# Splitting the q and k projections into fp16 halves straight from the matmul bank, in a two-layer graph attention kernel

## What is computed

```python
h = jnp.maximum(_layernorm(x, axis=-1), 0.0)
x = x + _L0_gnn_ref(h, adj, Wq, bq, Wk, bk, Wv, bv, beta)
h = jnp.maximum(_layernorm(x, axis=-1), 0.0)
x = x + _L1_gnn_ref(h, adj, Wq, Wk, Wv, bv, Wo, bo)
```

## Time and profile before

| | |
|---|---|
| median of 3 runs | 2788.24 us (2787.83 to 2789.91) |
| span of the profiled execution, first to last instruction | 2786.6 us |
| PE busy | 2492.9 us, 89% |
| VectorE busy | 2035.5 us, 73% |
| ScalarE busy | 2045.4 us, 73% |
| GpSimd busy | 1205.5 us, 43% |
| DMA, share of 16 engines | about a third, 90 GB/s |

### The profile page before, as it was taken

The page is one execution under the profiler, slowest core; times in us unless marked ns, Lnnn a source line. Parts: engine busy times, 40 slices in busy tenths (PEclk is TensorE's granted clock), DMA queues, the critical chain, the costliest instruction groups (busy, mean ns, idle before and its releaser), DMA issues.

```text
span 2786.6 us, 78169 instructions
## 1 busy us (share of the span) xinstructions
PE 2492.9 (89%) x20772; PEld 1447.7 (52%) x20772; DVE 2035.5 (73%) x10864; ACT 2045.4 (73%) x7824; POOL 1205.5 (43%) x1543
## 2 busy tenths in 40 slices
PE   3699999999999999999999999999999999999976
PEld 2355555555555555555555555555555555555543
DVE  3477777777777777777777777777777777777756
ACT  2577777777777777777777777777777777777765
POOL 1344444454444444444444444444444444444431
PEclk8899999999999999999999999999999999999988
DMA  3333333333333333333333333333333333333321
GB/s 118 90 89 87 93 94 87 95 102 86 88 96 86 94 103 86 86 97 87 94 102 88 85 99 86 94 100 89 83 99 88 95 98 90 82 99 91 78 55 45
DMA packets 164279, 251.27 MB, mean 90 GB/s; under 512 B 29776, under 2 KB 114768, under 8 KB 163920
## 3 DMA queue, kind: packets, MB, share of 16 engines
q1 hardware_dynamic: 163920, 248.11, 33.7%
HBM read 71.83 MB, written 25.17 MB: 35 GB/s over the span
## 4 chain that ended last, share of the span: by engine, by line
PE 45%; ACT 17%; DVE 16%; issue 16%; POOL 3%; SPq 1%; ACTq 1%; DVEq 1%; DMA 0%; POOLq 0%
PE job_bank L765 21%; ACT probs L479 12%; PE pt_bank L792 9%; PE o_bank L807 4%; PE misc_bank L832 4%; DVE neg L575 4%; PE score_bank L781 2%; PE misc_bank L846 2%; DVE stats L603 2%; ACT h_hi L516 2%; ACT probs_t L493 2%; PE misc_bank L868 1%; ACT qk L531 1%; DVE h_lo L700 1%; POOL part_lo L420 1%
## 5 line engine op out<-in xcount | busy, mean ns | idle before, releaser
L479 ACT ACTIVATE probs<-neg,neg_max 128x128 f32<-128x128 f32 x3072 | 1185.5, 390 | 9.4 <-DVE neg_max L575 9.4
L493 ACT ACTIVATE probs_t<-pt_bank 128x512 f32<-128x512 f32 x768 | 458.2, 597 | 567.7 <-PE pt_bank L792 516.5
L406 POOL TENSOR_TENSOR rstd<-shift_var,minus_half 128x1 f32<-128x1 f32 x256 | 152.2, 595 | 1020.3 <-DVE shift_var L612 1020.3
L479 ACT ACTIVATION_READ_ACCUMULATOR probs<-neg,neg_max 128x1 f32 x3072 | 583.9, 190 | 0.0
L792 PE MATMUL pt_bank<-ident,probs 128*128 128x128 f32 x3072 | 476.1, 278 | 57.5 <-ACT probs L479 42.9
L420 POOL TENSOR_TENSOR part_lo<-qk,part_hi 128x512 f16<-128x512 f32 x384 | 459.1, 1205 | 115.6 <-DVE part_hi L710 115.6
L792 PEld LDWEIGHTS pt_bank<-ident,probs 128*128 128x128 f32 x3072 | 362.7, 141 | 238.9 <-ACT probs L479 154.8
L765 PE MATMUL job_bank<-h_hi,w_hi 128*128 128x512 f16 x1152 | 441.4, 383 | 43.9 <-ACT qk L531 25.4
L765 PE MATMUL job_bank<-h_lo,w_hi 128*128 128x512 f16 x1152 | 438.5, 381 | 0.0
L765 PE MATMUL job_bank<-h_hi,w_lo 128*128 128x512 f16 x1152 | 438.0, 380 | 0.0
L575 DVE CUSTOM_DVE_ANT_0 neg<-score_bank,bias 128x128 f32<-128x128 f32 x1536 | 352.8, 285 | 103.3 <-issue 98.6
(11 more groups left out here) (69 smaller groups left out, 3949.8 us busy)
## 6 DMA issues: line engine op xcount, KB each, us to landing
stack<-part_hi SPq DMA_DIRECT2D x1024, 96.0 KB, 2.2
stack<-part_lo SPq DMA_DIRECT2D x512, 96.0 KB, 2.2
x_norm<-in_x SPq DMA_DIRECT2D x32, 768.0 KB, 4.5
x_res<-in_x SPq DMA_DIRECT2D x32, 768.0 KB, 4.7
out_x<-result SPq DMA_DIRECT2D x128, 192.0 KB, 1.9
adj<-in_adj SPq DMA_DIRECT2D x64, 256.0 KB, 2.9
stack<-in_L_gnn_Wq SPq DMA_DIRECT2D x2, 576.0 KB, 8.1
stack<-in_L_gnn_Wk SPq DMA_DIRECT2D x2, 576.0 KB, 8.9
```

What stands on the lines that cost most here:

```text
L406: pool.tensor_tensor(rstd[:, :], shift_var[:, b % 2, 1:2], minus_half[:, :], ALU.pow).then_inc(rstd_done, 1)
L479: last = act.activation(probs[c % 2][:, h, :], neg[c % 2][:, h, :], ACT.Exp, bias=neg_max[:, b, first + h:first + h + 1], scale=-1.0, accu ...
L493: act.activation(probs_t[c % 2][:, :, :].rearrange("p h q -> p (h q)"), pt_bank[c % 2][:, :], ACT.Copy).then_inc(probs_t_ready, 1)
```

## The change

q and k go from the bank to their halves without the fp32 copy. ACT writes the high half itself (scale and bias in the same instruction, output fp16), and DVE makes the low half in one instruction from the bank and the high half. GpSimd has no part in it. The bank is therefore free only when DVE is done: PE now waits on `part_lo_ready`. The wait for the landed copies moves from DVE to ACT. ACT no longer waits for the buffers of two jobs before. So that both engines form the same value in layer 0, where a bias is added, the weights of q and k are scaled by 16 instead of 256 and the factor is carried on: q and k are 16 times too large, the bias columns are scaled by 16, the scores are scaled back by 1/(256 sqrt(32)) inside the instruction of line 575, and beta and the mask value are scaled up to match. The setup gets two small DVE instructions more.

```diff
@@ GpSimd
-            def low_part(u, j):
-                n = u.n * 2 * KC + j
-                pool.wait_ge(part_hi_ready, n + 1)
-                pool.tensor_tensor(part_lo[j // KC][:, j % KC, :], qk32[j % 2][:, :],
-                                   part_hi[j // KC][:, j % KC, :], ALU.subtract).then_inc(part_lo_ready, 1)
...
-                    if p.project is not None and 2 <= s < 2 + 2 * KC:
-                        low_part(p.project, s - 2)
@@ ScalarE, slot j + 1
                         act.wait_ge(job_done, u.n * JOBS + (j + 1))
-                        if some(n - 1):
-                            act.wait_ge(part_hi_ready, n - 1)
-                        if some(n - 1):
-                            act.wait_ge(part_lo_ready, n - 1)
+                        if j % KC == 0 and some((u.half + u.parity) * STACK_DMAS * 16):
+                            act.wait_ge(stack_in[t][1 - u.parity], (u.half + u.parity) * STACK_DMAS * 16)
                         if u.layer == 0:
-                            last = act.activation(qk32[j % 2][:, :], job_bank[j % 2][:, :], ACT.Identity,
-                                                  scale=scale, bias=cols[:, j % KC:j % KC + 1])
+                            last = act.activation(part_hi[t][:, j % KC, :], job_bank[j % 2][:, :], ACT.Identity,
+                                                  scale=1.0, bias=b_cols[t][:, j % KC:j % KC + 1])
                         else:
-                            last = act.activation(qk32[j % 2][:, :], job_bank[j % 2][:, :], ACT.Copy, scale=scale)
-                        last.then_inc(qk32_ready, 1)
+                            scale = (SCALE[1] if t == 0 else 1.0) / W_SCALE
+                            last = act.activation(part_hi[t][:, j % KC, :], job_bank[j % 2][:, :], ACT.Copy,
+                                                  scale=scale)
+                        last.then_inc(part_hi_ready, 1)
@@ VectorE, slot j + 1
-                        dve.wait_ge(qk32_ready, u.n * 2 * KC + (j + 1))
-                        if j % KC == 0 and some((u.half + u.parity) * STACK_DMAS * 16):
-                            dve.wait_ge(stack_in[j // KC][1 - u.parity], (u.half + u.parity) * STACK_DMAS * 16)
-                        dve.tensor_copy(part_hi[j // KC][:, j % KC, :], qk32[j % 2][:, :]).then_inc(part_hi_ready, 1)
+                        t = j // KC
+                        dve.wait_ge(part_hi_ready, u.n * 2 * KC + (j + 1))
+                        if u.layer == 0:
+                            last = dve.scalar_tensor_tensor(part_lo[t][:, j % KC, :], job_bank[j % 2][:, :],
+                                                            b_cols[t][:, j % KC:j % KC + 1], part_hi[t][:, j % KC, :],
+                                                            ALU.add, ALU.subtract)
+                        else:
+                            scale = (SCALE[1] if t == 0 else 1.0) / W_SCALE
+                            last = dve.scalar_tensor_tensor(part_lo[t][:, j % KC, :], job_bank[j % 2][:, :], scale,
+                                                            part_hi[t][:, j % KC, :], ALU.mult, ALU.subtract)
+                        last.then_inc(part_lo_ready, 1)
@@ TensorE, first third of job j
-                        pe.wait_ge(qk32_ready, u.n * 2 * KC + (j - 1))
+                        pe.wait_ge(part_lo_ready, u.n * 2 * KC + (j - 1))
@@ VectorE, scores and setup
-                        scale=-1.0, scalar=HUGE, op0=ALU.add, op1=ALU.min,
+                        scale=(-1.0 / SCORE0 if u.layer == 0 else -1.0), scalar=HUGE, op0=ALU.add, op1=ALU.min,
...
-            dve.tensor_scalar(bq_cols[:, :], bq_raw[:, :], SCALE[0], None, ALU.mult).then_inc(bq_ready, 1)
+            for t in range(2):
+                dve.tensor_scalar(b_cols[t][:, :], b_raw[t][:, :], QK0_SCALE, None, ALU.mult).then_inc(cols_ready, 1)
+            dve.tensor_scalar(beta_all[:, :], beta_raw[:, :], SCORE0, None, ALU.mult).then_inc(cols_ready, 1)
+            dve.wait_ge(cols_ready, 3)
```

More of the change, by code:

```diff
@@ L46 @@
 SCALE = (float(HEAD) ** -0.5, float(DIM) ** -0.5)
+QK0_SCALE = 16.0
+SCORE0 = QK0_SCALE * QK0_SCALE / SCALE[0]
 class Unit:
@@ L175, in build @@
         carried_p, carried_v = count(), count()
+        beta_raw = sb("beta_raw", [P, 1])
         beta_all = sb("beta_all", [P, 1])
-        bq_raw = sb("bq_raw", [P, KC])
-        bq_cols = sb("bq_cols", [P, KC])
-        bk_cols = sb("bk_cols", [P, KC])
+        b_raw = [sb(f"b_raw{t}", [P, KC]) for t in range(2)]
+        b_cols = [sb(f"b_cols{t}", [P, KC]) for t in range(2)]
         bv_rows = [sb(f"bv_rows{m}", [P, DIM]) for m in range(2)]
@@ L201, in build @@
         h_lo = [sb(f"h_lo{b}", [P, KC, TOK], F16) for b in range(2)]
-        qk32 = [sb(f"qk32{b}", [P, TOK]) for b in range(2)]
         part_hi = [sb(f"part_hi{t}", [P, KC, TOK], F16) for t in range(2)]
@@ L245, in build @@
         half_ready = sem("half_ready")
-        bq_ready = sem("bq_ready")
+        cols_ready = sem("cols_ready")
         weight_turned = sem("weight_turned")
@@ L264, in build @@
         job_done = sem("job_done")
-        qk32_ready = sem("qk32_ready")
         part_hi_ready = sem("part_hi_ready")
@@ L308, in _ @@
         def _(sp):
-            sp.dma_start(bq_raw[:, :], b0q.rearrange("(c p) -> p c", p=P),
+            sp.dma_start(b_raw[0][:, :], b0q.rearrange("(c p) -> p c", p=P),
                          allow_slow_non_contiguous=True).then_inc(consts_in, 16)
-            sp.dma_start(bk_cols[:, :], b0k.rearrange("(c p) -> p c", p=P),
+            sp.dma_start(b_raw[1][:, :], b0k.rearrange("(c p) -> p c", p=P),
                          allow_slow_non_contiguous=True).then_inc(consts_in, 16)
-            sp.dma_start(beta_all[:, :], beta[0].partition_broadcast(P)).then_inc(consts_in, 16)
+            sp.dma_start(beta_raw[:, :], beta[0].partition_broadcast(P)).then_inc(consts_in, 16)
             sp.dma_start(x_norm[:, :, :], x_groups[0]).then_inc(x_norm_in, 16)
@@ L460, in _ @@
                 act.wait_ge(weight_in[m], 16)
-                act.activation(w_hi[m][:, :, :], staging(m), ACT.Copy, scale=W_SCALE).then_inc(w_hi_ready, 1)
+                act.activation(w_hi[m][:, :, :], staging(m), ACT.Copy,
+                               scale=QK0_SCALE if m < 2 else W_SCALE).then_inc(w_hi_ready, 1)
             for m in range(3, 7):
@@ L467, in _ @@
                                    scale=W_SCALE).then_inc(w_hi_ready, 1)
-            act.wait_ge(bq_ready, 1)
+            act.wait_ge(cols_ready, 3)
             act.wait_ge(consts_in, 96)
@@ L521, in phase @@
                         u, j = p.project, s - 1
-                        n = u.n * 2 * KC + j
+                        t = j // KC
                         act.wait_ge(job_done, u.n * JOBS + (j + 1))
-                        if some(n - 1):
-                            act.wait_ge(part_hi_ready, n - 1)
-                        if some(n - 1):
-                            act.wait_ge(part_lo_ready, n - 1)
-                        scale = (SCALE[u.layer] if j < KC else 1.0) / W_SCALE
+                        if j % KC == 0 and some((u.half + u.parity) * STACK_DMAS * 16):
+                            act.wait_ge(stack_in[t][1 - u.parity], (u.half + u.parity) * STACK_DMAS * 16)
                         if u.layer == 0:
-                            cols = bq_cols if j < KC else bk_cols
-                            last = act.activation(qk32[j % 2][:, :], job_bank[j % 2][:, :], ACT.Identity,
-                                                  scale=scale, bias=cols[:, j % KC:j % KC + 1])
-                        else:
-                            last = act.activation(qk32[j % 2][:, :], job_bank[j % 2][:, :], ACT.Copy, scale=scale)
-                        last.then_inc(qk32_ready, 1)
+                            last = act.activation(part_hi[t][:, j % KC, :], job_bank[j % 2][:, :], ACT.Identity,
+                                                  scale=1.0, bias=b_cols[t][:, j % KC:j % KC + 1])
+                        else:
+                            scale = (SCALE[1] if t == 0 else 1.0) / W_SCALE
+                            last = act.activation(part_hi[t][:, j % KC, :], job_bank[j % 2][:, :], ACT.Copy,
+                                                  scale=scale)
+                        last.then_inc(part_hi_ready, 1)
             run_phases(act, phase)
@@ L547, in _ @@
             dve.wait_ge(consts_in, 96)
-            dve.tensor_scalar(bq_cols[:, :], bq_raw[:, :], SCALE[0], None, ALU.mult).then_inc(bq_ready, 1)
+            for t in range(2):
+                dve.tensor_scalar(b_cols[t][:, :], b_raw[t][:, :], QK0_SCALE, None, ALU.mult).then_inc(cols_ready, 1)
+            dve.tensor_scalar(beta_all[:, :], beta_raw[:, :], SCORE0, None, ALU.mult).then_inc(cols_ready, 1)
+            dve.wait_ge(cols_ready, 3)
             for m in range(3):
                 dve.wait_ge(w_hi_ready, m + 1)
```

(6 more changed lines are left out.)

1 line of the change is left out of this document (added).

## The result

The changed kernel takes **2832.7 us** (median of 4, 2830.26 to 2836.19) against 2788.03 us for the kernel before in the same session: ratio **1.0162**, 95% interval 1.0148 to 1.0177. It is 1.6% slower. The forecast was 2819 us, with a range of 2786 to 2843. The granted clock was 0.985 of full speed on average in both profiled executions, so it has no part in the difference.

A forecast was written before the change was run, and what follows sets the result against it. PE, busy 89% of the span, was taken as the bound. Losses of 0.36 (phase A) and 0.67 (phase B) give 1.03 us per period, x 28 is 29, plus 2 outside the loop: 2819 us, range 2786 to 2843.

The forecast's parts named there:

- behind h_lo: Phase A, job 1: the bank comes free at 1064.81 against PE's start at 1064.45, so PE loses 0.36 us.
- job 4 hidden: Phase A: job 4 meets the same order, but PE waits for the exponentials in slot 6 anyway, so no loss.
- job 0: Phase B: PE loses about 0.2 us because job 0's bank comes free later.
- job 2's half behind VectorE's statistics: Phase B, slot 3: VectorE reaches job 2 late, so PE's job 4 starts 1.67 us later than before.
- ScalarE's half in fp16: ScalarE's fp16 output was to cost nothing: h_hi in fp16 took 0.474 us, o_t in fp32 0.471.
- the moved wait for the landed copies: On ScalarE instead of VectorE: to cost nothing, as the copies were made more than half a period before.
- The first rival: Removing GpSimd's work reaches the end: 1.31 us per period won, 2749 us; chance 0.10.
- Slots 7 and 8 of phase B: VectorE sets the pace: o_norm, and PE behind it, 0.73 + 0.28 - 0.34 = 0.67 us later.
- what POOL gives back: Phase B: without GpSimd's two part_lo beside it, the bias falls from 1.03 to 0.69 us, 0.34 back.
- The column operand: VectorE's new operation was priced from h_lo and w_lo at 0.69 us, with no separate term for a bias column.
- The upper bound of 1.08 us: VectorE's new operation, if held up beside GpSimd as the cast was in the worst row shown: 0.69 + 0.39 us.
- Outside the loop: The four phase pairs outside the loop have fewer engines in play: half the loss per period, 2 us.

The follow-up runs named there:

- e2_buf3: Kernel before, with three fp32 buffers for q and k in place of two: 2757.92 us, ratio 0.9891.
- e5_order: Changed kernel, with VectorE's part_lo of job 2 ahead of the norm's statistics in slot 3: 2819.77 us, ratio 1.0116.
- e8_buf3_bias: Kernel before with three fp32 buffers, and mask, scaled adjacency and bias moved from slot 7 to slots 1, 2, 4 of phase B: 2743.62 us.
- e1_gate: Kernel before, with PE taking the bank only after VectorE's cast (part_hi_ready in place of qk32_ready): 2835.23 us, ratio 1.0168.
- e7_gate3: Kernel before, with PE waiting for VectorE's cast and three fp32 buffers in place of two: 2831.94 us, ratio 1.0159.

## Why the prediction was right, and what was off

**The mechanism was right in phase A and up to job 6 of phase B.** Phase A was to lose 0.36 us behind h_lo, with job 4 hidden: it lost 0.33, nearly all in one slot. In phase B PE was to be 0.45, 1.67, 0.70 and 1.1 us late, counted up, for jobs 3, 4, 5 and 6: the table gives 0.46, 1.58, 0.60 and 1.01. Only job 0 was put too high, at 0.2 for 0.08. The wait that takes the place of the one on GpSimd is the one named, job 2's half behind VectorE's statistics. The operation took 0.688 us, estimated 0.69. ScalarE's half in fp16 cost nothing, and the moved wait for the landed copies is in no list of waits. The first rival (faster, 2749 us) named its own point of decision, VectorE being done with job 2 before 1023.15; it wasn't, and e2_buf3 shows what the rival's gain was worth where the bank isn't gated.

**The size was short: 31 us forecast, 45 measured.** A period loses 1.34 us and not 1.03, which is some 9 of the 14 us that are missing. Three terms were mis-sized.
- *Slots 7 and 8 of phase B.* The prediction let PE's 1.1 us fall to 0.67, because VectorE would get 0.34 back from the bias and set the pace. The bias did fall, from 1.03 to 0.69. But the mask just ahead of it rose from 0.42 to 0.79. From the start of the last half to the start of o_norm it took 1039.00 - 1035.29 = 3.71 us before and 4.05 after:

```profile
1051.81 0.74 DVE L703 SCALAR_TENSOR_TENSOR part_lo<-job_bank,b_cols,part_hi 128x512 f16<-128x512 f32 x1
...
1052.31 0.66 POOL L413 TENSOR_SCALAR normed<-x_mid,shift_var,rstd 128x384 f32<-128x384 f32 x1
...
1052.46 0.79 DVE L582 TENSOR_SCALAR mask<-adj 128x512 f32<-128x512 f32 x1
...
1055.86 0.55 DVE L678 TENSOR_TENSOR o_norm<-misc_bank,o_t 128x384 f32<-128x384 f32 x1
```

  The forecast was 0.06 less (0.28 for the longer operation, 0.34 off for the bias); measured is 0.34 more, so VectorE, and PE behind it, kept the full 1.0 us of job 6, and PE still idles 33.6 us in all for o_norm. The mask's 0.37 is most of the difference. In 9 of the 30 periods from the third mask on it kept 0.42 and the scaled adjacency took 0.73; there the distance is 3.94, and column 7 is 3.68 where it is 3.80 in the other 21. The step that failed is "what POOL gives back": it counted the collision that goes, and not that everything then shifts against GpSimd's norm and meets it elsewhere.
- *The column operand.* h_lo, the row that the duration was taken from, has a constant as its scalar; layer 0's part_lo has a column of bias, and took 0.06 us more. The upper bound of 1.08 us never came near, though it was not the worst of the trace: single casts of the kernel before took up to 1.31 us. By luck a release that is faster than I took it (0.06 us from VectorE's end to PE's start, not 0.12) made up for that.
- *Outside the loop.* I took 2 us. The third mask, the first of the loop, starts 3.4 us later than before (202.1 and 205.5), and the part behind the last mask is 1.5 us longer: 5 us. With 29 periods of 1.34 us this gives the 43.8 us by which the span grew.

## What to carry to other kernels

When two engines read a PSUM bank one after the other, the bank's release is set first by when the second comes to it in its own order, and only then by how long it takes: look what stands ahead of it in its list. A cheap copy that frees the bank early can be worth 75 us here, and the wait that it brought was cured by a third buffer (31 us) rather than by giving the copy up. Removing a wait wins only up to the next gate: the same buffer was worth 3 us where PE's next bank came free no earlier. And before an expensive instruction is moved into idle time on VectorE, look what GpSimd does in that stretch.

## What the runs showed of the hardware that was not expected

**VectorE and GpSimd stop each other, and the rows do not show who will pay.** In the changed kernel the mask, an fp32 operation from SBUF to SBUF, started 0.15 us behind GpSimd's norm and took 0.79 us for 0.42, ending 0.28 us after the norm did. That is so in 21 of the 30 periods from the third mask on. In the other nine of the same kernel the norm starts the same 0.15 us ahead (0.13 in the first), and the norm and the scaled adjacency are lengthened:

```profile
1306.87 0.94 POOL L413 TENSOR_SCALAR normed<-x_mid,shift_var,rstd 128x384 f32<-128x384 f32 x1
...
1307.02 0.42 DVE L582 TENSOR_SCALAR mask<-adj 128x512 f32<-128x512 f32 x1
...
1307.35 0.73 DVE L584 TENSOR_SCALAR scaled<-adj,beta_all 128x512 f32<-128x512 f32 x1
```

In e5_order the mask also started behind the norm, but kept its 0.42 us in all 30 periods:

```profile
1048.18 0.94 POOL L413 TENSOR_SCALAR normed<-x_mid,shift_var,rstd 128x384 f32<-128x384 f32 x1
1048.34 0.42 DVE L582 TENSOR_SCALAR mask<-adj 128x512 f32<-128x512 f32 x1
1048.67 0.73 DVE L584 TENSOR_SCALAR scaled<-adj,beta_all 128x512 f32<-128x512 f32 x1
```

Here the norm takes 0.94 for 0.66 and the scaled adjacency 0.73 for 0.47. With the same starts either one is lengthened, so the starts in the rows do not say who pays; what decides it was not tried. Among the largest cases are 1.56 us for 0.69 (e8_buf3_bias) and 1.38 and 1.43 for 0.43 (e1_gate, e7_gate3), all beside GpSimd's two-input subtraction. The Trainium skill (SBUF — State Buffer, "SBUF: two separate sides") has this as a lock on a shared port pair, which the one that starts first holds for a whole instruction. The traces agree in that one of two such neighbours stands still for most of the other's time (the cast of 1.38 us began 0.06 us behind the subtraction and ended 0.28 after it); that the first to start keeps its time they do not bear out by the starts in the rows, as the norm of 0.94 us shows. The profiler's times for GpSimd are rough, though, and whether a row's start is the moment at which the pair is taken no run here shows. By the same section an instruction of VectorE with at most one input in SBUF, outside the two-port modes, is outside the lock. The traces agree: part_lo, with one tensor in PSUM and one in SBUF, ran 678 to 693 ns with a constant and 740 to 752 ns with a column, in all 192 instances of each in the changed kernel, of which 93 and 124 ran beside a row of GpSimd.
